# Quantised attention: TensorE's order within a slot, from second, second, first, first to first, second, second, first

## The reference, cut to what matters

```python
def _L1_xattn_ref(x, cond, Wq, bq, Wkv, bkv, Wp, bp):      # x (2, 128, 256), cond (2, 2048, 256)
    H, hd = (16, 16)
    q = (x @ Wq + bq).reshape(1, B * N, H, hd)
    kv = (cond @ Wkv + bkv).reshape(1, -1, 2, H, hd)       # 4096 keys for all 256 queries
    ...
    q = _fq_sym(q, axis=-1)                                # rounded to 8-bit steps
    k = _fq_sym(k, axis=-1)
    v = _fq_sym(v, axis=2)
    attn = softmax(einsum('bhqd,bhkd->bhqk', q, k))
    attn = _fq_unsigned(attn, axis=-1)                     # rounded to 1/255 of the largest in its row
    out = einsum('bhqk,bhkd->bhqd', attn, v)
    return out @ Wp + bp
```

## Time and profile before

| | |
|---|---|
| median of three runs | 688.6 us (687.6 to 690.27) |
| the profiled execution | span 687.7 us, from its first to its last recorded instruction |
| PE busy | 651.0 us, 95% |
| DVE busy | 576.4 us, 84% |
| ACT busy | 417.5 us, 61% |
| POOL busy | 389.1 us, 57% |
| 256 reductions of first scores, L1892 | 159.6 us, 683 ns each, 20.7 us idle before them |
| 128 exponentials of second scores, L1885 | 153.5 us, 1204 ns each, 22.6 us idle before them |
| 512 matmuls of scores, L1843 | 140.4 us, 9.4 us idle before them |

### The profile page before, as it was taken

How to read it: one execution, slowest core, us unless ns; L and a number is a source line. 1 busy time by engine, 2 the same in 40 slices (tenths; PEclk the granted TensorE clock), 3 DMA queues, 4 the chain that set the end, 5 groups by cost and what they waited for, 6 DMA issues and landing times.

```text
span 687.7 us, 13890 instructions
## 1 busy us (share of the span) xinstructions
PE 651.0 (95%) x5088; PEld 410.1 (60%) x5088; DVE 576.4 (84%) x1029; ACT 417.5 (61%) x697; POOL 389.1 (57%) x500
## 2 busy tenths in 40 slices
PE   8899999999999999999999999999889889988887
PEld 6456766666666676766766666654436444544453
DVE  5998987887897797899989769888877889999655
ACT  5644454444544465565654445549878899899941
POOL 5876666566557736689965516526635543345401
PEclk9999999999999999999999999999989999999999
DMA  9666689765756588988974965639998899999900
GB/s 309 164 147 140 146 184 172 173 140 122 158 122 151 120 196 215 210 173 193 184 168 118 226 144 115 148 81 218 235 186 153 168 149 198 160 185 163 201 14 9
DMA packets 347827, 111.01 MB, mean 161 GB/s; under 512 B 313704, under 2 KB 344432, under 8 KB 347760
## 3 DMA queue, kind: packets, MB, share of 16 engines
q1 hardware_dynamic: 347760, 110.13, 77.1%
HBM read 31.97 MB, written 0.26 MB: 47 GB/s over the span
## 4 chain that ended last, share of the span: by engine, by line
PE 67%; DVE 21%; ACT 5%; issue 3%; DMA 2%; POOL 1%; DVEq 0%; ACTq 0%; POOLq 0%
PE psum L1060 21%; PE psum L1032 20%; DVE tops L1892 8%; PE psum L1843 6%; PE psum L1046 5%; PE psum L506 3%; ACT cT L1885 3%; DVE neg_max L1272 2%; PE psum L1908 2%; DMA c_nat<-cT 2%; PE psum L1085 1%; PE psum L1095 1%; PE psum L827 1%; PE psum L845 1%; DVE e_lo L1260 1%
## 5 line engine op out<-in xcount | busy, mean ns | idle before, releaser
L1060 PE MATMUL psum<-c_nat,eT 128*128 128x256 f16 x1536 | 188.1, 273 | 0.9 <-ACT u_sb L1234 0.9
L1892 DVE TENSOR_REDUCE tops<-psum 128x1 f32<-128x512 f32 x256 | 159.6, 683 | 20.7 <-PE psum L1843 20.1
L1885 ACT ACTIVATE cT<-psum,bias,q_scale 128x1024 f16<-128x1024 f32 x128 | 153.5, 1204 | 22.6 <-PE psum L1843 21.1
L1032 PE MATMUL psum<-cT,qk 128*128 128x512 f16 x744 | 165.6, 379 | 0.1
L1060 PEld LDWEIGHTS psum<-c_nat,eT 128*128 128x128 f16 x1536 | 147.3, 98 | 24.1 <-issue 1.6
L1843 PE MATMUL psum<-kT,v_space 128*128 128x512 f16 x512 | 140.4, 389 | 9.4 <-DVE tops L1892 7.3
L1032 PEld LDWEIGHTS psum<-cT,qk 128*128 128x128 f16 x744 | 72.6, 98 | 82.3 <-issue 1.2
L1272 DVE TENSOR_REDUCE neg_max<-psum 128x1 f32<-128x2048 f32 x32 | 73.2, 2287 | 21.3 <-PE psum L1032 21.2
L1260 DVE TENSOR_TENSOR e_lo<-e_all,e_hi 128x2048 f16<-128x2048 f32 x32 | 88.5, 2767 | 0.0
L1843 PEld LDWEIGHTS psum<-kT,v_space 128*128 128x128 f16 x512 | 45.4, 99 | 71.4 <-DVE tops L1892 34.4
L1203 ACT ACTIVATE e_all<-psum,neg_max 128x2048 f32<-128x2048 f32 x32 | 63.1, 1970 | 16.5 <-DVE neg_max L1274 16.4
(11 more groups left out here) (286 smaller groups left out, 947.3 us busy)
## 6 DMA issues: line engine op xcount, KB each, us to landing
wvo_h<-in_L_xattn_Wv SPq DMA_DIRECT2D x30, 128.0 KB, 2.4
wvo_h<-in_L_xattn_Wo SPq DMA_DIRECT2D x30, 128.0 KB, 2.3
wqk_h<-in_L_xattn_Wq SPq DMA_DIRECT2D x28, 128.0 KB, 2.4
wqk_h<-in_wkT SPq DMA_DIRECT2D x28, 128.0 KB, 2.6
mx_land<-in_mx_weights SPq DMA_DIRECT2D x8, 384.0 KB, 4.0
v_space<-in_ctx SPq DMA_DIRECT2D x4, 512.0 KB, 5.8
cT<-in_ctx SPq DMA_DIRECT2D x2, 1024.0 KB, 8.3
c_nat<-in_expert_wT SPq DMA_DIRECT2D x2, 1024.0 KB, 6.6
```

The source lines that it names most:

```text
L1032: ins = pe.matmul(s_ps[:, n * 512:(n + 1) * 512], c.qk[:, u % 2, q_part, k, :], m.cT[:, b, c_part, 4 * n:4 * n + 4, k, :], start=(k, q_par ...
L1060: ins = pe.matmul(u_ps, c.eT[:, v % 2, e_part, j, :], m.c_nat[:, v // H0, c_part, j, :], start=(j, e_part, c_part) == (0, 0, 0), stop=(j, ...
L1885: act.activation(m.y[:, u % 2, q * CHUNK:(q + 1) * CHUNK], m.bank(second_place(u, q), 2), ACT.Exp, bias=m.bias[:, u:u + 1], scale=m.q_scal ...
L1892: dve.tensor_reduce(m.tops[:, n // NB, n % NB:n % NB + 1], m.bank(n % 3), AX.X, ALU.max, negate=True).then_inc(s["q_max"], 1)
```

## The change

In each slot the two blocks of first scores no longer stand together behind the second scores. The first of them stands ahead of the two matmuls of second scores, the other behind them. The instructions are the same, and so are their waits, their banks and the other engines' lists. The kernel after is longer by two lines, so its lines beyond L1940 have numbers that are higher by two.

```diff
@@ -1931,11 +1931,13 @@
     pe.wait_ge(s["v_rounded_pool"], KT // 4)
     for u in range(1, UNITS + 2):
         for q in range(NC):
+            ahead = AHEAD + NB * u + 2 * q
+            if ahead < NB * UNITS:
+                pe_first(pe, m, s, ahead)
             if u < UNITS:
                 pe_second(pe, m, s, u, q)
-            for n in range(AHEAD + NB * u + 2 * q, AHEAD + NB * u + 2 * q + 2):
-                if n < NB * UNITS:
-                    pe_first(pe, m, s, n)
+            if ahead + 1 < NB * UNITS:
+                pe_first(pe, m, s, ahead + 1)
             if q == 0:
                 side.upto(NC * u - 0.5)
             if u >= UNITS and q < 2:
```

## The result

The changed kernel takes 690.43 us (median of 13 runs, 688.63 to 692.33); the kernel before took 688.43 us in 13 runs on the same chip. One of these 13 took 1316.21 us and stays out of the ratio. The ratio is 1.0034, with a 95% interval from 1.0022 to 1.0045: 2.3 us more (1.5 to 3.1); the two medians differ by 2.0 us. The interval is clear of no change, though the change is smaller than the 3.4 us that the prediction took as the least that can be told. The forecast was 690.4 us. Its time was right; of the steps behind it the largest was right, one was far too small, others were off the other way. One mark that it named went the other way, and one of its signs of being wrong, gaps in DVE in the second half, came. The profiled execution of the changed kernel has a span of 689.1 us, 1.4 us more than the one before.

A forecast was written before the change was run, and what follows sets the result against it. It took DVE as the bound from 561 to 647 us, PE from 518 to 536, nobody from 536 to 561. 687.7 + 1.05 + 0.84 + 1.50 - 1.55 = 689.5 us of span, with 0.9 around it 690.4 us; range 687.2 to 693.5.

The forecast's parts named there:

- gaps in DVE in the second half: Sign of a wrong forecast: DVE has gaps in the second half, where ACT's lag would then have reached it.
- The queries of the second batch: Slots (14, 1) and (14, 2): second scores behind blocks that wait delay ACT's copies and exponentials, 1.50 us more, the largest term.
- First blocks 0.43 us earlier: Four places on the chain where DVE waited for a slot's first block: gains of 0.43, 0.43, 0.43 and 0.26, together 1.55 us.
- the 0.26 us at 593 us: The smallest of the four gains from earlier first blocks: 0.26 us, no more than DVE's wait there.
- The product slots: Slots with expert or linear attention products: ACT has no slack, 0.21 us paid once per unit, four units, 0.84 us more.
- Exponentials later on the chain: Five exponentials on the chain of waits, 469.8 to 644.9 us, each 0.21 us later: 1.05 us more.
- The rival of the low clock: TensorE's clock stays low longer after the queries' copies, twelve matmuls cost 2.5 us more: 692.9 us; chance 0.23.
- DVE's waits: Rival: DVE's twenty waits for first scores, 483 to 561 us, each fall by 0.43 us: 8.6 us less, 680.0 us; chance 0.09.
- the gap on ACT: Sign: the exponential behind the first copy of the queries starts about 0.9 us after that copy's end instead of at once.
- DVE's waits below 13.5 us in the first half: Sign: DVE's waits for first scores fall below 13.5 us in the first half.
- a DVE nearly as full in the second: Sign: in the second half DVE is as full as before, 83.4 of 86 us.
- ACT's waits for second scores: Sign: ACT's waits for second scores rise from 7.5 us in the second half.

The follow-up runs named there:

- Pair: New order only in slots (14, 1) and (14, 2), old order elsewhere, against the kernel before: 690.19 us, ratio 1.0023.
- late: New order only in the slots after (14, 2), old order elsewhere, against the kernel before: 688.82 us, ratio 1.0008.
- gap: New order only in slots (14, 3) to (19, 0) and unit 28, against the kernel before: 687.97 us against 688.29, ratio 0.9989.
- after: The changed kernel itself, new order in all slots, against the kernel before: 690.43 us, ratio 1.0034.
- early: New order only in the slots before (14, 2), old order from there on, against the kernel before: 688.21 us, ratio 1.000.
- all but spot: New order everywhere but in slot (14, 2), against the kernel before: 689.10 us, ratio 1.001.
- busy: The changed kernel plus four products that compute nothing on PE ahead of block 128's wait for the queries' copy: 690.98 us, ratio 1.003 against the kernel before.
- Products: New order only in slots (9, 1) to (11, 3), those of the experts' products, against the kernel before: 688.52 us, ratio 0.9999.
- dilated: New order only in slots (19, 1) to (21, 2), those of the dilated attention, against the kernel before: 688.43 us, ratio 0.9999.
- feed: New order only in slots (24, 1) to (30, 2), those of the feed-forward layer, against the kernel before: 688.93 us against 689.23, ratio 1.0003.
- spot: New order only in slot (14, 2), that of block 128, against the kernel before: 689.14 us, ratio 1.0012.

## Why the prediction was right, and where it was not

**The queries of the second batch, +1.50 us: right.** Pair has 1.38 us on ACT's last copy, step by step as forecast: first exponential 1.06 (1.08 in the forecast), first copy 0.38 (0.50), next exponential 1.37 (1.50), and a gap of 0.92 us (0.9). In the changed kernel's trace the same place is blurred by the clock.

**First blocks 0.43 us earlier, -1.55 us: about right where it can be read.** Behind the queries I took 0.43 us; late and gap show 0.31. For the 0.26 us at 593 us the changed kernel has 0.21, right behind a loss of 0.37. Of the two places ahead of 548 us, the second shows. From 513.3 to 548.3 us the kernels with the new order all the way win 0.22 to 0.24 us (after, early, all but spot, and busy, which goes from -1.31 to -1.53). Products alone lose 0.28 us there, so the rest of the new order wins about 0.5 us. But the wait that goes is not the one at 538.92 us that I had named (0.69 us, 0.64 in the changed kernel): it is the next. DVE in the kernel before:

```profile
544.84 1.29 DVE L1892 TENSOR_REDUCE tops<-psum 128x1 f32<-128x512 f32 x2 [0.52 <-PE psum L1843]
```

In the changed kernel the same two reductions are the last of seven that follow each other:

```profile
540.82 4.47 DVE L1892 TENSOR_REDUCE tops<-psum 128x1 f32<-128x512 f32 x7
```

The first place, at 480 us, had 0.17 us (DVE -0.17 at 480.15 us), and what came of it can't be told. Behind it stands the wait for a DMA at 503 us, and in the eight kernels with the old order up to there it ends from 0.07 us earlier to 0.92 us later than in the kernel before.

**The product slots, +0.84 us: too much.** 0.29 us for three units (products), and for the products of the linear attention nothing that stays: ACT was up to 0.48 us later there (474.8 us, by the same subtraction) and nearly level again at 486 us (0.07). It is the same lag handed on over the units, too, not only within one.

**Exponentials later on the chain, 5 x 0.21 = 1.05 us: this step failed, by its count.** Two of the five lie ahead of 500 us, and what they cost is lost in the scatter of the wait for the DMA. The prediction had put that DMA's part at nothing, and no run here shows its size. The other three, with the 0.26 us against them, should have made 0.63 - 0.26 = 0.37 us between 569 and 648 us; late has 1.22, the changed kernel 1.21, dilated and feed 0.51 and 0.62 one by one. I had counted the exponentials that the chain of waits names. But each piece that goes from ACT to DVE stands behind an exponential too. Before, such a piece was just in time (a wait of 0.18 us or none), and so on no chain. In feed three such rounds cost 0.21 us each, which is as much as its whole loss (0.62). It was in the prediction that a delay of ACT could open gaps in DVE, as a mark of being wrong; it should have been a term.

**The rival of the low clock** (0.23) was half there. In the changed kernel it fell at 551.6 us, and cost 1.74 - 1.12 = 0.62 us: DVE lost 0.83 + 0.91 = 1.74 us from 548 to 569 us, the order alone makes 0.40 + 1.03 - 0.31 = 1.12. But the low clock of the kernel before at 557.86, 0.91 us, was gone, and the one at 503 us was shorter. So clock and order mix in the two spans. The order's sum from 513.3 to 648 us is -0.23 + 1.12 + 1.21 = 2.10 us. The timed runs give 2.3 (1.5 to 3.1), and 2.1 at equal clock. The forecast had 1.84 us. The mean granted clock of the timed runs, 0.9963 in the 13 of the changed kernel and 0.9966 in the 35 of the kernel before beside early, leaves the clock next to no part in the timed difference. Two readings of mine were wrong without weight for the sum: in the kernel before the clock was not back after the four matmuls at 557.86 (the one at 559.74 us still took 0.63 us instead of 0.39), and one of the seven exponentials of the tail, at 648.21 us, waited 0.37 us for PE. **DVE's waits** (faster) fell by 1.6 us from 483 to 561 us, not by 8.6.

**Of the marks,** the gap on ACT, DVE's waits below 13.5 us in the first half (11.9) and a DVE nearly as full in the second (82.7 instead of 83.4 of 86 us) are as forecast. ACT's waits for second scores should have risen and fell (4.8 instead of 7.5 us). I take it that idle time is the lag of PE less how late ACT comes to it, and that ACT came later because DVE, which frees the banks, was late as well; no run shows this apart. Part of it is the label, too: all idle time ahead of the exponentials fell only from 7.8 to 7.2 us. It is a poor mark for a lag.

That the time was right is partly luck. A missed loss of 0.84 us in the second half stood against 0.43 us between 513 and 548 us (+0.20 in the forecast, -0.23 in the traces) and 0.20 us ahead of 503 us of which nothing can be told. With 0.07 us less at the queries and 0.12 us less gain behind them, the forecast was short of the traces by 0.26 us.

## What to carry to other kernels

When a step is moved back, list what is handed on by the engine behind it to the engine that is full, and look up for each how early it is in the trace: those with no slack and no wait are on no chain and become waits first. A wait in an in-order list belongs behind everything that doesn't need it; one block in the wrong place made 1.0 of the 2.1 us. And compare two traces by the start times of the same instruction, not by spans or idle times: it showed 0.3 us where a dozen timed runs can't tell 1 us. And sort timed runs by their granted clock before you compare them.

## What the runs showed of the hardware

TensorE's clock fell at different places in executions in which PE did the same or nearly the same. Behind the wait for a DMA near 503 us, 2.43 us long in the kernel before and in dilated, where the order is the old one in both, the granted clock from 500 to 512 us was 0.72 in the one and 1.00 in the other; in eight others, the changed kernel among them, it was 0.86. Here is dilated's wait:

```profile
503.68 0.56 PE L1908 MATMUL psum<-v_space,c_nat 128*128 128x16 f16 x16 [2.43 <-DMA c_nat<-cT]
```

Behind the last copy of the queries PE waited 2.09 us in spot and the clock stayed at 1.00; in pair it waited 2.09 us too and it fell (0.76 from 556 to 562 us). In the kernel before it fell after 1.55 us, in feed it did not after 1.56. So the length of the wait didn't tell here whether the clock falls behind it. Spot's stretch, with the clock third from the right:

```profile
556.00:562.00 6.00, 5.24 (x54) 2.82 (x55) 4.11 (x9) 5.97 (x12) 2.92 (x7) 1.00 0.82 140
```

A stretch at low clock is worth 0.6 to 1.1 us here (0.62 in the changed kernel, 0.91 in the kernel before, 1.03 in pair, 2.26 - 1.12 = 1.14 in busy), as much as each term that I had worked out; none of these traces shows what tells the executions apart. The Trainium skill, TensorE: Matmul & The Clock Gate, says in Part 1 that the interval over which the chip judges PE's activity runs freely and doesn't start with the kernel, so that the moment of a change differs from run to run. The traces agree in so far as the same wait stands before either outcome (2.43 us, there with the same order too, and 2.09 us); each kernel was traced in one execution.
